# Turning 2,048 normalised tokens: 64 TensorE transposes replaced by 16 DMA transposes of two bf16 parts

## The reference

```python
x = x + 0.5 * ffn(layernorm(x))
h = layernorm(x)                       # the tokens that are turned
q, k, v, gate = h @ Wq.T, h @ Wk.T, h @ Wv.T, h @ Wg.T
dt = softplus(h @ Win.T + dt_bias)     # chunks of 128 tokens, decay from cumsum(-dt*A)
y = intra-chunk + inter-chunk attention; y = y / rms * gnorm_w * silu(gate)
x = x + y @ Wo.T
x = x + 0.5 * ffn(layernorm(x))
```

## Time and profile before

| what | value |
|---|---|
| median of 3 runs | 1642.57 us (1641.81 to 1643.51) |
| the profiled execution's own time | 1642.75 us |
| its span, first to last instruction | 1640.9 us |
| granted TensorE clock, mean | 0.989 of full speed |
| busy share: PE / DVE / ACT / POOL | 97% / 83% / 67% / 86% |
| DMA engines, hardware queue | 29.7% |

### The profile page before, as it was taken

One profiled execution on the slowest core, in us unless ns is written; L12 is line 12 of the kernel. 1 busy time (PEld: TensorE's weight loads), 2 busy tenths in 40 slices (PEclk: granted clock), 3 DMA queues, 4 the chain that ended last, 5 costly groups with the idle time before them and its releaser, 6 DMA issues.

```text
span 1640.9 us, 33589 instructions
## 1 busy us (share of the span) xinstructions
PE 1589.4 (97%) x11028; PEld 883.8 (54%) x11028; DVE 1368.9 (83%) x2945; ACT 1093.0 (67%) x2987; POOL 1411.7 (86%) x1316
## 2 busy tenths in 40 slices
PE   7898999999999999999999999999999999999986
PEld 5554555555555555555555555555555555555554
DVE  6988788888878888787878888788888878788876
ACT  4666677676766677766766667666776667666653
POOL 4767899888988899888998989888998889888974
PEclk8999999999999999999999999999999999999998
DMA  5123233232333223231332224323342224322222
GB/s 211 39 55 67 55 74 87 65 72 52 78 85 78 53 59 102 54 83 47 91 78 64 61 64 92 72 72 53 73 95 59 72 46 97 72 65 52 53 45 103
DMA packets 208012, 118.76 MB, mean 72 GB/s; under 512 B 173792, under 2 KB 174816, under 8 KB 206816
## 3 DMA queue, kind: packets, MB, share of 16 engines
q1 hardware_dynamic: 207840, 116.63, 29.7%
HBM read 70.19 MB, written 4.46 MB: 45 GB/s over the span
## 4 chain that ended last, share of the span: by engine, by line
PE 74%; POOL 11%; DVE 8%; issue 4%; ACT 2%; DMA 0%; ACTq 0%; POOLq 0%; DVEq 0%
PE B L325 23%; PE B L323 23%; PE B L324 23%; POOL QS L1410 2%; POOL ROWS L1423 2%; POOL RR L1456 1%; DVE WL L1696 1%; POOL PL L1445 1%; PE B L553 1%; POOL ZS L1449 1%; POOL WVF L1433 1%; POOL K L1417 1%; POOL WVL L1441 1%; POOL RM L1453 1%; DVE PF L1640 1%
## 5 line engine op out<-in xcount | busy, mean ns | idle before, releaser
L323 PE MATMUL B<-WH,XTH 128*128 128x128 bf16 (+1 forms) x992 | 269.3, 296 | 0.6 <-DVE QF L1610 0.6
L324 PE MATMUL B<-WL,XTH 128*128 128x128 bf16 (+1 forms) x992 | 269.3, 296 | 0.0
L325 PE MATMUL B<-WH,XTL 128*128 128x128 bf16 (+1 forms) x992 | 269.3, 296 | 0.0
L1410 POOL TENSOR_TENSOR QS<-QS,SIN 128x512 f32<-128x512 f32 x160 | 219.3, 1371 | 42.8 <-ACT QS L1137 42.7
L323 PE MATMUL B<-XTH,WH 128*128 128x512 bf16 x640 | 243.2, 380 | 1.0 <-DVE G L1630 1.0
L325 PE MATMUL B<-XTH,WL 128*128 128x512 bf16 x640 | 243.3, 380 | 0.0
L324 PE MATMUL B<-XTL,WH 128*128 128x512 bf16 x640 | 243.2, 380 | 0.0
L1689 DVE SCALAR_TENSOR_TENSOR YF<-B,RR,G 128x128 f32<-128x128 f32 x512 | 144.2, 344 | 113.4 <-POOL RR L1456 113.3
L1169 ACT ACTIVATE PF<-ROWS,NG 128x128 f32<-128x128 f32 x512 | 162.7, 389 | 79.1 <-POOL ROWS L1423 78.8
L1449 POOL TENSOR_TENSOR ZS<-YF,ZS 128x512 bf16<-128x512 f32 x128 | 158.0, 1235 | 64.5 <-ACT ZS L1207 64.2
L1136 ACT ACTIVATE QS<-B 64x512 f32<-64x512 f32 x160 | 94.9, 593 | 150.3 <-PE B L325 143.5
(11 more groups left out here) (209 smaller groups left out, 4320.9 us busy)
## 6 DMA issues: line engine op xcount, KB each, us to landing
ROWS<-rows_dram SPq DMA_DIRECT2D x128, 256.0 KB, 3.2
STAGE<-in_wall SPq DMA_DIRECT2D x108, 256.0 KB, 2.8
ACC<-in_x SPq DMA_DIRECT2D x3, 1024.0 KB, 10.0
out<-ACC SPq DMA_DIRECT2D x3, 1024.0 KB, 3.9
ZT<-ZS SPq DMA_TRANSPOSE x128, 3.1
ACC<-in_x SPq DMA_DIRECT2D x4, 256.0 KB, 3.6
COS<-in_cos SPq DMA_DIRECT2D x1, 1024.0 KB, 12.0
SIN<-in_sin SPq DMA_DIRECT2D x1, 1024.0 KB, 14.7
```

The source lines that it names most:

```text
L323: nc.tensor.matmul(out_, ah, bh, start=first, stop=False)
L324: nc.tensor.matmul(out_, ah, bl, start=False, stop=False)
L325: return nc.tensor.matmul(out_, al, bh, start=False, stop=last)
L1410: nc.gpsimd.tensor_tensor(QS[:, sl, :], QS[:, sl, :], SIN[:, t0:t0 + TB], ALU.mult).then_inc(sin_ready.sem, 1)
```

## The change

The second turn no longer goes through PE and PSUM. ACT normalises into `XN`, now two fp32 buffers; ACT rounds it to bf16 into the first half of `XS` (two buffers, both parts side by side: 128x1024 bf16); DVE subtracts in SBUF into the second half; and one DMA transpose per chunk, issued by SP, turns both parts into `XT`, of which `XTH` and `XTL` are now views. `T_PARTS` (the order in which the three PSUM banks are used) loses its 16 "second" entries.

```diff
-        XTH = sb("XTH", [P, KT, L], BF16)
-        XTL = sb("XTL", [P, KT, L], BF16)
+        XT = sb("XT", [P, 2, KT, L], BF16)
+        XTH, XTL = XT[:, 0, :, :], XT[:, 1, :, :]
...
-                ("GN", [P, 1], F32), ("XN", [P, BLK, HID], F32)))
+                ("GN", [P, 1], F32), ("XN", [P, 2, HID], F32), ("XS", [P, 2, 2, HID], BF16)))
...
+        x_turned = [Sem(f"x_turned{i}", 2) for i in range(2)]
...
+        def turned_at(f, i):
+            return 16 * x_turned[i % 2].at(f, i // 2)
...
-            for i in range(6, PO + 2):
-                load_piece(0, i, 0)
+            def turn_tokens(f, chunks=range(BLK)):
+                for i in chunks:
+                    sp.wait_ge(f_xl.sem, f_xl.at(f, i))
+                    t = f * TB + i * P
+                    sp.dma_start_transpose(XT[:, :, :, t:t + P].rearrange("p a k t -> p (a k) t"),
+                                           XS[:, i % 2, :, :].rearrange("p a e -> p (a e)")).then_inc(x_turned[i % 2].sem, 16)
+
+            turn_tokens(0)
+            load_piece(0, 6, 0)
+            load_piece(0, 7, 0)
+            turn_tokens(1, (0,))
+            load_piece(0, 8, 0)
+            turn_tokens(1, (1, 2, 3))
+            load_piece(0, 9, 0)
+            load_piece(0, 10, 0)
+            turn_tokens(2)
+            load_piece(0, 11, 0)
+            turn_tokens(3)
...
-                if f:
-                    act.wait_ge(f_tp2.sem, f_tp2.at(f - 1, i))
-                nc.scalar.activation(XN[:, i, :], A[:, i, :], ...
+                if f or i >= 2:
+                    act.wait_ge(f_xl.sem, f_xl.at(f, i - 2))
+                nc.scalar.activation(XN[:, i % 2, :], A[:, i, :], ...
...
+        def act_normal_hi(act, f, chunks=range(BLK)):
             for i in chunks:
+                act.wait_ge(f_xn.sem, f_xn.at(f, i))
+                if f or i >= 2:
+                    act.wait_ge(x_turned[i % 2].sem, turned_at(f, i - 2))
+                nc.scalar.activation(XS[:, i % 2, 0, :], XN[:, i % 2, :], ACT.Copy).then_inc(f_xh.sem, 1)
+
+        def dve_normal_lo(dve, f, chunks=range(BLK)):
+            for i in chunks:
+                dve.wait_ge(f_xh.sem, f_xh.at(f, i))
+                nc.vector.tensor_tensor(XS[:, i % 2, 1, :], XN[:, i % 2, :], XS[:, i % 2, 0, :], ALU.subtract).then_inc(f_xl.sem, 1)
...
         def pe_dt(pe, f):
...
-                pe.wait_ge(f_xtl.sem, f_xtl.at(f, i))
+                pe.wait_ge(x_turned[i % 2].sem, turned_at(f, i))
```

More of the change, by code:

```diff
@@ L48 @@
 EARLY_AFTER = {2: 0, 3: 1, 4: 2, 5: 3, 7: 4, 8: 6, 9: 7}
-T_PARTS = (("turn", 0, 0, 4), ("turn", 1, 0, 4), ("turn", 2, 0, 4), ("second", 0, 0, 4), ("turn", 3, 0, 2), ("dt", 0, 0, 1), ("turn", 3, 2,
-           2), ("second", 1, 0, 4), ("dt", 1, 0, 1), ("second", 2, 0, 4), ("dt", 2, 0, 1), ("second", 3, 0, 4), ("dt", 3, 0, 1))
+T_PARTS = (("turn", 0, 0, 4), ("turn", 1, 0, 4), ("turn", 2, 0, 4), ("turn", 3, 0, 2), ("dt", 0, 0, 1), ("turn", 3, 2, 2),
+           ("dt", 1, 0, 1), ("dt", 2, 0, 1), ("dt", 3, 0, 1))
 T_ORDER = [(kind, f, first + i) for kind, f, first, count in T_PARTS for i in range(count)]
@@ L293, in build @@
         f_wt, f_wtc, f_mix, f_acc = (Sem(n, k) for n, k in (("f_wt", 1), ("f_wtc", 1), ("f_mix", 4), ("f_acc", 4)))
-        f_tp2, f_xth, f_xtl = (Sem(n, 4) for n in ("f_tp2", "f_xth", "f_xtl"))
+        f_xh, f_xl = (Sem(n, 4) for n in ("f_xh", "f_xl"))
+        x_turned = [Sem(f"x_turned{i}", 2) for i in range(2)]
         f_part, f_added = Sem("f_part"), Sem("f_added")
@@ L708, in act_normalise @@
             for i in chunks:
-                if f:
-                    act.wait_ge(f_tp2.sem, f_tp2.at(f - 1, i))
-                nc.scalar.activation(XN[:, i, :], A[:, i, :], ACT.Identity, bias=NMR[:, 1, f % 2, i:i + 1],
+                if f or i >= 2:
+                    act.wait_ge(f_xl.sem, f_xl.at(f, i - 2))
+                nc.scalar.activation(XN[:, i % 2, :], A[:, i, :], ACT.Identity, bias=NMR[:, 1, f % 2, i:i + 1],
                                      scale=RSTD[:, 1, f % 2, i:i + 1]).then_inc(f_xn.sem, 1)
-        def pe_turn2(pe, f, chunks=range(BLK)):
+        def act_normal_hi(act, f, chunks=range(BLK)):
             for i in chunks:
[L717 to L723, removed]
-            for i in chunks:
[L725 to L734, removed]
+                act.wait_ge(f_xn.sem, f_xn.at(f, i))
[3 more added lines that the diff above has]
+        def dve_normal_lo(dve, f, chunks=range(BLK)):
+            for i in chunks:
+                dve.wait_ge(f_xh.sem, f_xh.at(f, i))
+                nc.vector.tensor_tensor(XS[:, i % 2, 1, :], XN[:, i % 2, :], XS[:, i % 2, 0, :], ALU.subtract).then_inc(f_xl.sem, 1)
         def pe_dt(pe, f):
@@ L1003, in _ @@
             pe_dt(pe, 0)
-            pe.wait_ge(f_xtl.sem, f_xtl.at(0, BLK - 1))
+            for i in (2, 3):
+                pe.wait_ge(x_turned[i % 2].sem, turned_at(0, i))
             fill(0, 0, 0, None, True, 0)
@@ L1031, in _ @@
             pe_dt(pe, 2)
-            pe_turn2(pe, 3, (0,))
             pe_sums(pe, 0)
-            pe_turn2(pe, 3, (1,))
+            fill(0, 0, 8, None, True, 0)
             pe_rows(pe, 0)
-            pe_turn2(pe, 3, (2, 3))
             pe_sums(pe, 1)
             pe_dt(pe, 3)
-            fill(0, 0, 8, None, True, 0)
             pe.wait_ge(d_in.sem, d_in.at(NB - 1, 0))
@@ L1265, in _ @@
             act_normalise(act, 2, (0,))
+            act_normal_hi(act, 2, (0,))
             hi(0, 0, 0)
             act_normalise(act, 2, (1,))
+            act_normal_hi(act, 2, (1,))
             act_dt_exp(act, 0)
             swap(0, 0, 4, 4)
[L1270 removed]
+            act_normalise(act, 2, (2,))
+            act_normal_hi(act, 2, (2,))
+            act_normalise(act, 2, (3,))
+            act_normal_hi(act, 2, (3,))
             split_hi(0, 9)
[L1272 removed]
             hi(0, 0, 1)
```

64 lines of the change are left out of this document (27 added, 37 removed).

## The result

| | before | after |
|---|---|---|
| time, median (us) | 1642.76 (1641.81 to 1643.51, 4 runs) | 1666.58 (1665.56 to 1669.95, 4 runs) |
| ratio to before | | 1.0149, 95% interval 1.0131 to 1.0166 |
| profiled execution: span (us), granted clock | 1640.9, 0.989 | 1664.8, 0.979 |

The change makes the kernel 23.8 us slower; 1665 was forecast. Lines of the changed kernel's functions carry new numbers: the subtraction is L743 (before L733), the rounding on ACT L738, the normalisation L730, the transpose on SP L389.

What follows compares the result with a forecast made beforehand. DVE's list in the prologue, not PE, was taken as the bound up to the first `decayed`; eight steps summed to 22.8 us, less 0.4 for fewer meetings with POOL, giving 1665 us, range 1656 to 1674.

Steps and rivals of the forecast that it cites:

- the prediction's heading: In the prologue, the added cost was headed a DMA round trip inside a ring of two buffers, 3.8 us with rounding.
- Steps 1 to 6: DVE's list from block 0's third subtraction to dt of block 2: delays accumulate from 2.1 to 15.9 us.
- Step 2: Block 2's first mix: late landing, then fill 0 on PE at low clock; adds 2.0 us, shift 4.1.
- Step 3: Block 1's ring wait holds a swap and block 3's router weights on ACT, delaying block 3's first mix; adds 5.0 us.
- Step 7: Block 3's subtractions: ring wait, and the last behind turned sums, now behind fill 8; adds 3.9 us, ending at 111.0.
- Step 8: Prologue's tail: last dt waits for DMA and PE, putting the first `decayed` at 120.5; adds 3.0 us, shift 22.8.
- The removal of 64 transposes from PE: On PE in the prologue: 8 us of work removed, but worth nothing, since DVE ends PE's idle time.
- Rival A: The loop's start swallows part of the delay through PE's 6.4 us wait near 138 us: 1658.6 us; chance 8%.
- Rival B: The 16 DVE subtractions meet POOL on the shared port: +3.7 us at the median, +13.4 at worst; chance 10%.
- Rival C: DMA transposes land late, one us more on each of five round trips: 1670 us; chance 10%.
- Rival D: PE was the bound: the round trip is hidden and 8 us of PE work come back, 1635 us; chance 2%.
- The low-clock terms: PE's fills 0, 3 and 6 run at low clock after rests: 1.1, 0.9 and 1.7 us, possibly absent.

Runs made afterwards that it cites:

- e1: The changed kernel with four buffers instead of two for XS, which the transposes read, XN still two: 1660.32 us, ratio 1.0113.
- e4: The changed kernel with ACT taking block 1's second swap and block 3's router weights ahead of the last normalisation and rounding of block 1: 1665.76 us, ratio 1.0150.
- e5: The changed kernel with fill 8 on PE moved back behind the dt of block 3, as before the change: 1668.43 us, ratio 1.0160.
- e2: The changed kernel with four buffers for the fp32 XN, XS still two: 1666.18 us, ratio 1.0148.
- e3: The changed kernel with four buffers in both rings, XN and XS: 1659.62 us, ratio 1.0110.
- e6: The changed kernel plus unwanted matmuls (12, 28, 38, 14) in four rests of PE, to keep its clock up: 1666.59 us, ratio 1.0151.
- e7: e3 with fill 8 moved back, dt of block 1 and fill 3 behind block 3's mixes, and block 3's normalisations, roundings and subtractions earlier: 1651.89 us, ratio 1.0064.
- e11: The kernel before the change plus unwanted matmuls (9, 4, 14) in PE's first three rests: 1639.07 us, ratio 0.9987.
- e9: e7 with piece 6 loaded between block 0's transposes and block 2's first two chunks made earlier on ACT, DVE and POOL: 1654.67 us, ratio 1.0081.
- e10: e9 plus unwanted matmuls (9, 4, 14) in PE's first three rests, ahead of the change's place: 1651.62 us, ratio 1.0059.
- e12: e7 plus unwanted matmuls (9, 4, 14) in PE's first three rests: 1651.01 us, ratio 1.0054.

## Why the prediction was right

The time, 1666.6 for 1665, is right, and so is the mechanism: a DMA round trip of 3.2 us, inside a ring of two and again at the readers, on the engine that never rested. The weights within it are not those of the prediction's heading: with the ring removed only 6 to 7 of the 23.8 us go, since the waits of the readers take its place.

The steps, against the earlier trace rows. After's DVE list starts 1.9 us earlier (35.79 against 37.68). That is not the change's doing: two other forms of the changed kernel, e1 and e4, start at 37.92 and 38.11 (the last section has all of them). So what the change itself did is the shift plus 1.9:

| step | shift predicted | shift in the profile | plus 1.9 |
|---|---|---|---|
| 1. third subtraction of block 0 | 2.1 | 0.5 | 2.4 |
| 2. first mix of block 2 | 4.1 | 2.5 | 4.4 |
| 3. first mix of block 3 | 9.1 | 7.8 | 9.7 |
| 4. series | 10.6 | 9.2 | 11.1 |
| 5. last subtraction of block 2 | 14.3 | 12.5 | 14.4 |
| 6. dt of block 2 | 15.9 | 14.3 | 16.2 |
| 7. last subtraction of block 3, end | 19.8 | 20.0 | 21.9 |
| 8. first `decayed` | 22.8 | 23.95 | 25.8 |

- Steps 1 to 6 are each right within 0.6 us. Round trips lasted nearly as priced: from the end of subtraction i-2 to the start of subtraction i about 4.1 us in block 0, 4.0 in block 1 and 3.8 in block 3 (3.8 predicted), with landings of 3.2. No pair stands closer.
- Step 2's order of causes and its size held: 1.11 us waited for PE at the mix.
- Step 3: size right. Its path on ACT, a swap and the router weights behind the rounding, is real but worth only 1.1 us, and without it the time is the same (e4).
- Step 7 is mis-sized: its term in the sum, 3.9 us, measured 5.7. ACT in order of time shows the place:

```profile
105.77 0.63 ACT L738 ACTIVATE XS<-XN 128x512 bf16<-128x512 f32 x1 [1.80 <-DMA XT<-XS]
108.43 0.28 ACT L843 ACTIVATE CONST<-B 128x128 f32<-128x128 f32 x1 [2.03 <-PE B L837]
108.60 0.62 ACT L1138 ACTIVATE QH<-QF 128x512 bf16<-128x512 f32 x1
109.12 0.80 ACT L730 ACTIVATE XN<-ACC,NMR,RSTD 128x512 f32<-128x512 f32 x1
```

  The copy of the turned sums (L843) waits for PE, which runs fill 8 at a granted 0.59 (104 to 108 us); normalisation, rounding and subtraction of chunk 3 are behind it. The prediction named fill 8 but gave it no price of its own: it had the last subtraction end 2.4 us after the one ahead of it (111.0 against 108.6), and measured are 4.2. e5 took 2.1 us out of this piece by moving fill 8 alone.
- Step 8 is mis-sized by 0.9 (3.0 in the sum, 3.95 measured): L792 and L793 took 1.33 and 1.35 us, and their counterparts in the kernel before 1.52 and 0.28. POOL adds the mask to ROWS from 118.60 to 121.27 in this profile, just then; before, it did so from 94.48 to 96.98, beside the first of the two alone (at 95.73). In e5 POOL starts that at 119.47, and the same two instructions, at 118.01 and 118.35, take 0.42 and 0.29. The Trainium skill (SBUF — State Buffer, "SBUF: two separate sides") says that certain DVE operations, those with two SBUF inputs among them, and GpSimd's take the shared ports by turns, a whole instruction each; these pairs agree with it.
- The two mis-sized terms (2.7 us) were in part covered by the 1.9 us of the earlier start, so the profiled time came out closer than the sum deserved: 25.8 us of the change's own against 22.4 forecast. That is luck.
- The removal of 64 transposes from PE, priced at nothing, fits the busy time of e1 and e2, 0.8 and 0.6 us below the kernel before, but no run tests it alone.
- Rival A fell: shift at `decayed` and shift of the end are equal. Rival B fell for the subtractions: 692 ns at the median, 862 at worst. Rival C fell: landings 3.0 to 3.3. Rival D fell twice: after, and in e3, where the buffers are not waited for and the time is still 18 us above before.
- The low-clock terms: 0.7 and 1.35 us in e6's profile for 0.9 and 1.7. But they are not visible in its time. The third, 1.1 us in step 2, is not worked out in the prediction, and no run shows it: in e6 the first mix of block 2 comes 18.7 us after the first subtraction, in after 18.1.

Where the 23.8 us are, by what took them away, each version against its own set's runs of before: 5.9 the ring (e3), 8.5 the order, by which readers meet less of the latency (e7 against e3), and 9.4 that are left in e7. In the profiles, counted from the first subtraction to the first `decayed`, the same parts are 8.7, 6.9 and 10.2 of 25.8 us. No version removed the last part by other means than early filling, from which the kernel before gains as well (e11), so its cause is in part open. In e7 it is spread: the last dt still waits 2.63 us, and dt of block 1, now behind the mixes, is 6.1 us later than before and the series behind it starts 5.65 us later (79.91 against 74.26).

## What to carry to other kernels

A transfer that takes the place of work on an engine that has time to spare saved nothing here and added its latency, where a ring waited for it and again at its readers. Before giving a transfer a ring of N buffers, compare its round trip (here 3.8 us with the rounding) with the time between step i and i-N on the busiest engine (here 1.2 us). More buffers take away the wait in the ring (some 6 of 23.8 us), and only earlier work the wait of the readers. And look at the granted clock in a prologue: cheap matmuls in PE's first rests gained 1.9 us (0.13%) in a kernel whose PE was 97% busy.

## What the runs showed of the hardware that was not expected

**The low clock ends at different times in runs of the same instructions.** Up to the first subtraction of block 0 the kernels before, after, e1 to e7 and e9 give DVE the same work, and PE too, but for four transposes at 33.5 us in the kernel before. After rests in 12 to 16 us PE's clock is at 0.50 (1.2 GHz) for all or part of 16 to 20 us (0.50 to 0.74 on average), and in their profiles it comes back either before or after 24 us:

| granted clock in 20 to 24 us | profiles | start of the first subtraction (us) |
|---|---|---|
| 0.50 | before, e1, e4, e6 | 37.68, 37.92, 38.11, 37.32 |
| 0.76 to 1.00 | after, e2, e3, e5, e7, e9 | 35.79, 34.69, 35.90, 35.32, 35.89, 35.43 |
| 1.00, rests filled | e10, e11, e12 | 34.37, 33.97, 34.32 |

Between the first two rows of the table lie 1.4 to 3.4 us, with the same work up to there. That is as much as several steps of the prediction, so steps must be compared from a common start. The Trainium skill (TensorE: Matmul & The Clock Gate, Part 1) says that the clock's rise is run-variable; the table agrees.

**The clock can stay low while PE has no rest.** In e9's rows above PE is busy 4.00 of 4.00 us from 36 to 44 us, most of it with the router's 128x64 fp32 matmuls, and the clock stays at 0.50; in after it was 1.00 from 36 to 40 us with the same work. The 24 router matmuls of that stretch took 5.22 us in e9 and 2.79 in after. Where it had been up already, in e10, it stayed up through them. What decides it was not found.
